# Mixture-of-experts layer, one core: the shared layer of the first four token tiles moved into the second router's tail, in plain fp32

## The chip, the cores and the metric

One core of a Trainium2 chip runs the whole program. The metric is the device time of one execution in microseconds (us), lower is better. TensorE is called PE here, its weight loads PEld, VectorE DVE, ScalarE ACT, GpSimd POOL and SyncE SP. PE's clock has two levels, 2.4 GHz (the profile writes 1.00) and 1.2 GHz (0.50).

## The reference

The input is 16 images of 16 x 16 pixels with 256 channels, so 4096 tokens. Four residual layers follow one another: a spectral mix, a first mixture of experts (gated, top 2 of 8), an attention-like convolution, and a second mixture of experts. Only the last one is touched:

```python
# h: the normalised tokens, 4096 x 256
logits = x @ w_router.T                          # 8 experts
expert_weight, expert_idx = top_k(softmax(logits), 2)
...
inter = square(relu(binned @ w1[e].T))           # each chosen expert, 256 hidden
moe_out = ...scatter of (inter @ w2[e].T) * expert_weight...
sh = square(relu(h @ ws1.T))                     # shared layer, 512 hidden, every token
shared_out = sh @ ws2.T
x = x + shared_out + moe_out
```

## The kernel before

Tokens are held in 32 tiles of 128 rows. `x_res` keeps the residual in SBUF (128 x 256 floats a tile, `x_tile(j)`), and the normalised tokens are written to DRAM twice: as rows (`h_rows`) and turned, channels on partitions (`h_turned`, `ht_dram`). The attention stage writes both, and ends at about 798 us of the profile. From there to the end the kernel has three parts, each a block of its own with a barrier of all engines at its end.

**The second router's tail** (`router_tail("moe1", ...)`, L425 to L543). DVE selects the two best experts, counts tokens per expert, and gives every (token, choice) a slot. Then a loop over 8 batches of 4 tiles and 2 choices builds the table that says which token sits in which slot: DVE compares against a ramp (L527, L529), ACT scales the tile part with the token number (L468, 64 instructions of 128 x 72), and PE adds up 64 products of 128 x 128 by 72 columns in `ids_ps` (L482). Rings are two deep: DVE waits for `s_spread` of two batches before, ACT for `s_equal`, PE for `s_one_hot`. L485 closes the sum, L541 and L543 turn it into integers. SP has one job here, `late`: the load of the 2 MB `down1_raw` (L2382). Before the loop PE does three small products (L475 to L477), and then waits for ACT.

**The second experts** (`mlp("experts1", ...)`), 71 slots of 128 rows. At its start SP loads the first two groups of turned tokens for the part after it (L871), and at its end PE does the first two products of the shared layer (`SharedLead.EARLY`).

**The shared layer and the output** (`SharedLead` L849 and `shared` L899). Every operand is split in a high and a low fp32r half, and each product is made as three (`product`, L176, whose matmuls are L182 to L184). Tokens go in groups of 4 tiles: SP loads 512 KB of `h_turned` a group (L871), ACT and DVE split it (L879, L187), PE projects it in 4 products of 512 columns (6 matmuls each), ACT applies relu, square and the copy of the high half (L966, L968, L972), DVE makes the low half (L187), and PE projects back tile by tile (12 matmuls of 256 columns). PE's order is written out by hand: `project_back(t)`, then `project(t + LEAD)`, with `LEAD = 6`; `project_back(t)` waits until `add_y(t - 4)` has emptied its bank. POOL gathers the two expert rows of each token, two gathers a tile, 64 in all (L923), into a ring of `DEPTH = 8` buffers; a gather waits until the sum of eight gathers before is done. DVE adds the gathers to the residual (`add_routed`, L998, 2 a tile) and then the shared result (`add_y`, L1004). Its order is by hand as well:

```python
for t in range(TILES):
    add_y(t)
    c = t + LEAD
    low_a(c)
    add_routed(t + AHEAD_Y)      # AHEAD_Y = 4
```

SP stores a tile when `add_y` is through (L935). Each DVE wait stands in this order, so a late gather holds up the additions behind it.

Of the kernel before, what the change touches and what calls it, by code (L numbers as in the profile page):

```python
# [23 lines left out]
P = 128  # L24
# [3 lines left out]
KC = C // P  # L28
# [78 lines left out]
def build(nc, A, out):  # L107
    _, where = constants()
    ctx = ExitStack()
    with ctx:  # L110
# [314 lines left out]
        def router_tail(tag, choice, logits, late=None):  # L425

            BATCH = 4
            with ExitStack() as tail:  # L428
# [16 lines left out]
                at_tile = [[sb(f"{tag}_at_tile{k}{b}", [P, BATCH * TABLE_T], HALF, on=tail) for b in range(RING)] for k in range(2)]  # L445
                block = tail.enter_context(nc.Block())
# [7 lines left out]
                if late is not None:  # L454
                    @block.sync
                    def _(sp):
                        late(sp)

                @block.scalar
                def _(act):  # L460
                    act.wait_ge(s["apart"], 1)
                    nc.scalar.activation(share[:, :], apart[:, :], ACT.Exp).then_inc(s["exp"], 1)
                    for n in range(TILES // BATCH):
                        for k in range(2):
                            act.wait_ge(s_equal[k], n + 1)
                            for i in range(BATCH):
                                part = at_tile[k][n % RING][:, i * TABLE_T:(i + 1) * TABLE_T]
                                last = nc.scalar.activation(part, part.bitcast(F32), ACT.Copy, scale=token[:, n * BATCH + i:n * BATCH + i + 1])  # L468
                            last.then_inc(s_one_hot[k], 1)

                @block.tensor
                def _(pe):
                    pe.wait_ge(s["totals"], 1)
                    totals = count[:, :].rearrange("p (e j) -> p e j", e=E)[:, :, TILES - 1]
                    nc.tensor.matmul(sums_ps[:, 0:E], K("before"), totals, start=True, stop=True)  # L475
                    nc.tensor.matmul(sums_ps[:, E:2 * E], K("ones"), totals, start=True, stop=True).then_inc(s["bases"], 1)
                    nc.tensor.matmul(ids_ps[:, :], K("ident"), zeros[:, :], start=True, stop=False)  # L477
                    for n in range(TILES // BATCH):
                        for k in range(2):
                            pe.wait_ge(s_one_hot[k], n + 1)  # L480
                            for i in range(BATCH):
                                last = nc.tensor.matmul(ids_ps[:, :], at_row[k][n % RING][:, i * P:(i + 1) * P],  # L482
                                                        at_tile[k][n % RING][:, i * TABLE_T:(i + 1) * TABLE_T], start=False, stop=False)
                            last.then_inc(s_spread[k], 1)
                    nc.tensor.matmul(ids_ps[:, :], K("ident"), zeros[:, :], start=False, stop=True).then_inc(s["filled"], 1)  # L485
                    pe.wait_ge(s["words"], 1)
                    nc.tensor.matmul(words_ps[0:1, 0:WORDS], etile[:, :], K("words"), start=True, stop=True).then_inc(s["packed"], 1)

                @block.vector
                def _(dve):  # L490
# [40 lines left out]

                    dve.wait_ge(s["exp"], 1)
# [6 lines left out]
                    nc.vector.tensor_scalar(etile[:, :], etile[:, :], float(E - 1), None, ALU.min).then_inc(s["words"], 1)  # L539
                    dve.wait_ge(s["filled"], 1)  # L540
# [308 lines left out]
        class SharedLead:  # L849

            GROUP = 4
            GROUPS = TILES // GROUP
# [12 lines left out]
            def load(self, sp, g):  # L865
                if g >= self.GROUPS:
                    return
                if g >= RING:
                    sp.wait_ge(self.s["h_low"], g - RING + 1)
                width = KC * self.N  # L870
                sp.dma_start(self.hT_raw[g % RING][:, :], ht_dram[:, g * width:(g + 1) * width]).then_inc(self.s_raw[g % RING], 16)  # L871
# [27 lines left out]
        def shared(lead, ws2):  # L899

            GROUP, GROUPS, KI, N = lead.GROUP, lead.GROUPS, lead.KI, lead.N
            LEAD = KI + 2
            DEPTH = 8
            AHEAD_Y = DEPTH // 2
            with ExitStack() as on:  # L905
# [22 lines left out]
                def _(sp):  # L928
                    for g in range(RING, 2 * RING):
                        lead.load(sp, g)  # L930
                    for g in range(GROUPS):
                        lead.load(sp, g + 2 * RING)
                        for t in range(g * GROUP, (g + 1) * GROUP):
                            sp.wait_ge(s["added"], t + 1)
# [4 lines left out]
                def _(pe):  # L939
# [14 lines left out]
                    for t in range(TILES):  # L954
# [25 lines left out]
                def _(dve):  # L980
# [20 lines left out]
                    def add_y(t):  # L1001
                        dve.wait_ge(s["down"], t + 1)
                        dve.wait_ge(s["sum"], t * 2 + 2)
                        nc.vector.tensor_tensor(x_tile(t), x_tile(t), bankY[t % GROUP][:, 0:C], ALU.add).then_inc(s["added"], 1)  # L1004

                    for c in range(LEAD):
                        low_a(c)
                        if c >= LEAD - AHEAD_Y:
                            add_routed(c - LEAD + AHEAD_Y)
                        if c == KI - 1:  # L1010
                            lead.low_h(dve, RING)
                    for t in range(TILES):
# [3 lines left out]
                        add_routed(t + AHEAD_Y)  # L1016
# [1363 lines left out]
        with routing:  # L2380
            router_tail("moe1", choice, by_token(logits1, PARTS[1]),
                        lambda sp: sp.dma_start(down1_raw[0][:, :], A["L1_ffn_w2_stack"]).then_inc(loads["down1"], 16))  # L2382
# [72 lines left out]
```

## Time and profile before

| | us |
|---|---|
| median of 3 runs | 1080.37 (1078.08 to 1084.45) |
| the profiled execution, its own time | 1077.55 |
| its span, first to last instruction | 1075.7 |
| PE, DVE, ACT, POOL busy | 917.6, 609.9, 551.9, 271.2 |

The profile is of one execution. The stages named in the prediction are stretches of its span: the router's tail from 798 to 829 us, the experts from there to about 981, the shared layer from 981 to the end.

### The profile page before, as it was taken

How to read it: one execution, taken by the hardware profiler on the slowest of the kernel's cores; microseconds unless marked ns; L12 is line 12 of the kernel's file. 1: busy time of each engine (PE TensorE's matmuls, PEld its weight loads, DVE VectorE, ACT ScalarE, POOL GpSimd, SP SyncE). 2: the span in 40 equal slices, each digit the busy share in tenths (PEclk: the TensorE clock that was granted, in tenths of full speed). 3: DMA queues.
4: the chain of work that ended last, by engine and by line, in shares of the span. 5: the costliest groups of instructions: out<-in, count | busy, mean ns of one | idle time of the engine just before them, and what ended most of it. 6: DMA issues, size and time to landing. Idle time of an engine off the chain costs nothing. (4 is left out here: it accounts for less than half of the span.)

```text
span 1075.7 us, 20700 instructions
## 1 busy us (share of the span) xinstructions
PE 917.6 (85%) x6102; PEld 785.6 (73%) x6102; DVE 609.9 (57%) x1702; ACT 551.9 (51%) x1372; POOL 271.2 (25%) x274
## 2 busy tenths in 40 slices
PE   5656569999999999997378999998746899998998
PEld 3544458888888888886256777776625899997998
DVE  6887942332323323222777778767768555555786
ACT  6346543443434434343355555554436566667774
POOL 0000031121211212110763220000001544443775
PEclk9858569999999999999589999998655899999999
DMA  9655211111111111111843221102241344444654
GB/s 385 271 193 198 81 40 55 54 55 54 50 54 55 55 54 50 55 44 66 270 128 98 60 79 60 40 21 79 79 157 42 116 138 139 137 133 131 182 163 148
DMA packets 62231, 114.79 MB, mean 107 GB/s; under 512 B 9586, under 2 KB 43012, under 8 KB 60996
## 3 DMA queue, kind: packets, MB, share of 16 engines
q1 hardware_dynamic: 48900, 77.77, 20.5%
q0 software_dynamic: 12960, 35.41, 11.6%
q8 instruction: 58, 0.95, 0.4%
q10 hardware_dynamic: 288, 0.47, 0.1%
q14 instruction: 25, 0.20, 0.1%
HBM read 74.01 MB, written 39.59 MB: 106 GB/s over the span
## 5 line engine op out<-in xcount | busy, mean ns | idle before, releaser
L600 POOL DMA_INDIRECT experts_rows_sb<-h_rows,choices x142 | 137.5, 969 | 651.9 <-POOLq L428 325.9
L799 DVE TENSOR_TENSOR experts_a_sb<-experts_a_sb,experts_bankU 128x512 f32<-128x512 f32 x71 | 48.9, 689 | 223.1 <-PE experts_bankU L184 223.1
L747 ACT ACTIVATE experts_a_sb<-experts_bankG 128x512 f32<-128x512 f32 (+1 forms) x142 | 69.7, 491 | 90.4 <-PE experts_bankG L184 90.3
L760 ACT ACTIVATE experts_y_sb<-experts_bankY 128x256 f32<-128x256 f32 x142 | 54.7, 385 | 86.1 <-PE experts_bankY L181 66.6
L738 ACT ACTIVATE experts_hT<-experts_bankH 128x256 fp32r<-128x256 f32 x142 | 54.2, 382 | 80.5 <-PE experts_bankH L663 80.4
L1198 POOL DMA_INDIRECT attn_y<-y_rows,choices x64 | 65.6, 1024 | 108.3 <-DVE x_res L1652 55.9
L182 PE MATMUL experts_bankY<-down_high,experts_aT 128*128 x284 | 91.5, 322 | 0.3 <-DVE experts_aT L187 0.3
L183 PE MATMUL experts_bankY<-down_low,experts_aT 128*128 x284 | 79.8, 281 | 0.0
L184 PE MATMUL experts_bankY<-down_high,experts_aT 128*128 x284 | 79.8, 281 | 0.0
L923 POOL DMA_INDIRECT shared_y<-y_rows,choices x64 | 67.9, 1061 | 37.8 <-POOLq L555 18.5
L181 PE MATMUL experts_bankY<-down_plain,experts_aT_plain 128*128 x284 | 72.9, 379 | 0.0
L187 DVE TENSOR_TENSOR experts_aT<-experts_bankA,experts_aT 128x256 fp32r<-128x256 f32 x142 | 59.6, 420 | 22.9 <-ACT experts_aT L755 22.9
L670 PE MATMUL experts_bankA<-konst_sb,experts_a_sb 128*128 128x128 f32 x426 | 69.7, 273 | 1.7 <-DVE experts_aT L187 1.7
L663 PE MATMUL experts_bankH<-konst_sb,experts_rows_sb 128*128 128x128 f32 x284 | 55.7, 278 | 16.8 <-issue 14.2
L182 PE MATMUL experts_bankG<-gate_high,experts_hT 128*128 x142 | 69.6, 490 | 0.0
L187 DVE TENSOR_TENSOR experts_hT<-experts_bankH,experts_hT 128x256 fp32r<-128x256 f32 x142 | 59.8, 421 | 9.1 <-ACT experts_hT L738 9.0
L799 DVE TENSOR_TENSOR experts_a_sb<-experts_a_sb,experts_bankG 128x256 f32<-128x256 f32 x71 | 29.9, 421 | 56.1 <-ACT experts_a_sb L747 56.1
L663 PEld LDWEIGHTS experts_bankH<-konst_sb,experts_rows_sb 128*128 128x128 f32 x284 | 37.3, 142 | 27.3 <-issue 18.3
L183 PE MATMUL experts_bankG<-gate_low,experts_hT 128*128 x142 | 56.6, 398 | 0.0
L184 PE MATMUL experts_bankU<-up_high,experts_hT 128*128 x142 | 55.8, 393 | 0.0
L184 PE MATMUL experts_bankG<-gate_high,experts_hT 128*128 x142 | 55.7, 393 | 0.0
L182 PE MATMUL experts_bankU<-up_high,experts_hT 128*128 x142 | 55.6, 392 | 0.0
(367 smaller groups left out, 2626.4 us busy)
## 6 DMA issues: line engine op xcount, KB each, us to landing
y_rows<-experts_y_sb SPq DMA_DIRECT2D x142, 128.0 KB, 1.9
h_rows<-xn SPq DMA_DIRECT2D x32, 256.0 KB, 2.2
mix_xT<-in_xt SPq DMA_DIRECT2D x4, 1024.0 KB, 12.0
x_res<-in_x SPq DMA_DIRECT2D x4, 1024.0 KB, 13.9
gate_raw<-in_L_ffn_gate_w SPq DMA_DIRECT2D x2, 2048.0 KB, 13.6
up_raw<-in_L_ffn_up_w SPq DMA_DIRECT2D x1, 4096.0 KB, 25.1
x_rows<-x_res SPq DMA_DIRECT2D x16, 256.0 KB
x_res<-x_rows SPq DMA_DIRECT2D x8, 512.0 KB, 4.7
```

The source lines that it names most:

```text
L181: return nc.tensor.matmul(out, left[0], right[0], start=start, stop=stop)
L182: nc.tensor.matmul(out, left[0], right[0], start=start, stop=False)
L183: nc.tensor.matmul(out, left[0], right[1], start=False, stop=False)
L184: return nc.tensor.matmul(out, left[1], right[0], start=False, stop=stop)
L187: return eng.tensor_tensor(low, whole, high.bitcast(F32), ALU.subtract)
L600: nc.gpsimd.indirect_dma_start(rows[t % DEPTH][:, :], None, h_dram, bass.IndirectOffsetOnAxis(ap=ids_i[:, t:t + 1], axis=0)).then_inc(s_ro ...
L663: last = nc.tensor.transpose(bankH[:, kc * P:(kc + 1) * P], rows[i % DEPTH][:, kc * P:(kc + 1) * P], K("ident"))
L670: last = nc.tensor.transpose(bankA[:, k * P:(k + 1) * P], a_sb[i % RING][:, k * P:(k + 1) * P], K("ident"))
L747: nc.scalar.activation(a_sb[i % RING][:, :], bankG[i % RING][:, 0:hidden], ACT.Silu if gate is not None else ACT.Relu).then_inc(s["act"], 1)
L799: nc.vector.tensor_tensor(a_sb[i % RING][:, :], a_sb[i % RING][:, :], bankU[i % RING][:, 0:hidden], ALU.mult).then_inc(s["a"], 1)
L923: nc.gpsimd.indirect_dma_start(routed[u % DEPTH][:, :], None, y_dram, bass.IndirectOffsetOnAxis(ap=pos_i[:, t + k * TILES:t + k * TILES + ...
L1198: nc.gpsimd.indirect_dma_start(y_in[u % Y_RING][:, :], None, y_dram, bass.IndirectOffsetOnAxis(ap=pos_i[:, j + k * TILES:j + k * TILES + 1 ...
```

## The change

The four first tiles no longer go through `shared`. A new class `SharedEarly` computes their shared layer inside `router_tail` of the second router, from `h_turned` and from `ws1` and `ws2` in plain fp32 (not split), and adds it to `x_res` there. `shared` then handles 28 tiles; it still gathers and adds the expert rows of all 32 and stores the first four as soon as both sums are done. `AHEAD_Y` goes from 4 to 1, counted now from tile 4, so that DVE adds the expert rows five tiles ahead of the shared result of the same loop index.

```diff
+        class SharedEarly:
+            GROUP = 4
+            KI = IS // P
+            N = GROUP * P
+            PRODUCTS = GROUP * KI
...
+            def load(self, sp):
+                sp.dma_start(self.hT[:, :], ht_dram[:, 0:KC * self.N]).then_inc(self.s["hT"], 16)
+                sp.dma_start(self.ws1[:, :], A["L1_ffn_ws1"]).then_inc(self.s["ws1"], 16)
+                sp.dma_start(self.ws2[:, :], A["L1_ffn_ws2"]).then_inc(self.s["ws2"], 16)
+            def project(self, pe, k):
+                if k == 0:
+                    pe.wait_ge(self.s["hT"], 16)
+                    pe.wait_ge(self.s["ws1"], 16)
+                if k >= RING:
+                    pe.wait_ge(self.s["relu"], k - RING + 1)
+                for kc in range(KC):
+                    last = nc.tensor.matmul(self.bankU[k % RING][:, :], self.ws1[:, kc * IS + k * P:kc * IS + (k + 1) * P],
+                                            self.hT[:, kc * self.N:(kc + 1) * self.N], start=(kc == 0), stop=(kc == KC - 1))
+                last.then_inc(self.s["up"], 1)
+            def project_back(self, pe, first, end):
+                for j in range(first, min(end, self.PRODUCTS)):
+                    t, k = j // self.KI, j % self.KI
+                    if j == 0:
+                        pe.wait_ge(self.s["ws2"], 16)
+                    if t == 0:
+                        pe.wait_ge(self.s["square"], k + 1)
+                    last = nc.tensor.matmul(self.bankY[t // 2][:, t % 2 * C:(t % 2 + 1) * C], self.a[k][:, t * P:(t + 1) * P],
+                                            self.ws2[:, k * C:(k + 1) * C], start=(k == 0), stop=(k == self.KI - 1))
+                    if k == self.KI - 1:
+                        last.then_inc(self.s["down"], 1)
+            def activate(self, act, k):
+                act.wait_ge(self.s["up"], k + 1)
+                nc.scalar.activation(self.a[k][:, :], self.bankU[k % RING][:, :], ACT.Relu).then_inc(self.s["relu"], 1)
+                act.wait_ge(self.s["relu"], k + 1)
+                nc.scalar.activation(self.a[k][:, :], self.a[k][:, :], ACT.Square).then_inc(self.s["square"], 1)
+            def add(self, dve, b):
+                dve.wait_ge(self.s["down"], 2 * b + 2)
+                nc.vector.tensor_tensor(x_tile(2 * b, n=2), x_tile(2 * b, n=2), self.bankY[b][:, :], ALU.add)
...
 SP   +                        if early is not None:
+                            early.load(sp)
                         late(sp)
 ACT, after Exp and before the loop over n
+                        early.activate(act, 0)
+                        early.activate(act, 1)
 ACT, at the end of an iteration
+                        if early is not None and n in (1, 2):
+                            early.activate(act, n + 1)
 PE, after L477 and before the loop
+                        early.project(pe, 0)
+                        early.project(pe, 1)
 PE, at the start of an iteration
+                            if n in (1, 2):
+                                early.project(pe, n + 1)
+                            elif n > 2:
+                                early.project_back(pe, (n - 3) * 4, (n - 2) * 4)
 DVE, after the last comparison                    +  early.add(dve, 0)
 DVE, after L539, before the wait for the table    +  early.add(dve, 1)
...
 class SharedLead
-            GROUPS = TILES // GROUP
+            FIRST = SharedEarly.GROUP
+            GROUPS = (TILES - FIRST) // GROUP
...
 def shared
-            AHEAD_Y = DEPTH // 2
+            AHEAD_Y = 1
 SP
+                    for t in range(FIRST):
+                        sp.wait_ge(s["sum"], t * 2 + 2)
+                        sp.dma_start(out[t * P:(t + 1) * P, :], x_tile(t)).then_inc(s["stored"], 16)
 PE
-                    for t in range(TILES):
+                    for t in range(COUNT):
                         project_back(t)
                         lead.project(pe, t + LEAD)
 DVE
                     for c in range(LEAD):
                         low_a(c)
-                        if c >= LEAD - AHEAD_Y:
-                            add_routed(c - LEAD + AHEAD_Y)
+                        if c >= LEAD - FIRST:
+                            add_routed(c - LEAD + FIRST)
...
-                    for t in range(TILES):
+                    for t in range(AHEAD_Y):
+                        add_routed(FIRST + t)
+                    for t in range(COUNT):
                         add_y(t)
                         c = t + LEAD
                         low_a(c)
-                        add_routed(t + AHEAD_Y)
+                        add_routed(FIRST + t + AHEAD_Y)
```

## Rows read from the trace of the kernel before

**Rows 1.** The page, the span in 40 slices: granted clock of PE in tenths.
```profile
PEclk9858569999999999999589999998655899999999
```
**Rows 2.** Stretch, us; PE, PEld, DVE, ACT, POOL busy; clock, DMA share, GB/s.
```profile
797.00:804.00 7.00, 0.22 (x1) 0.00 (x0) 4.54 (x23) 0.00 (x0) 0.00 (x0) 0.50 0.51 173
...
812.00:828.00 16.00, 15.65 (x65) 14.85 (x65) 14.93 (x36) 15.02 (x62) 0.00 (x0) 0.50 0.00 0
...
836.00:842.00 6.00, 4.66 (x21) 3.86 (x20) 3.10 (x6) 2.87 (x6) 3.33 (x4) 0.50 0.27 70
```
**Rows 3.** Groups of instructions, 795 to 840 us: count, busy us, mean ns, idle before.
```profile
L468 ACT ACTIVATE moe_at_tile<-moe_at_tile,moe_token 128x72 fp32r<-128x72 f32 x64 | 15.8, 339 | 6.5 <-DVE moe_at_row L529 6.5
L482 PE MATMUL moe_ids<-moe_at_tile,moe_at_row 128*128 128x72 f32 x64 | 15.8, 413 | 6.4 <-ACT moe_at_tile L468 6.4
```
**Rows 4.** Timeline of the router's tail: start us, duration us, instruction.
```profile
799.94 0.34 SPq L2382 DMA_DIRECT2D down_raw<-in_L_ffn_w_stack  x1
...
805.32 0.68 PE L477 MATMUL moe_ids<-moe_zeros,konst_sb 128*128 128x72 f32 x2
...
811.21 10.91 ACT L468 ACTIVATE moe_at_tile<-moe_at_tile,moe_token 128x72 fp32r<-128x72 f32 x44 [6.46 <-DVE moe_at_row L529]
...
825.05 0.68 DVE L529 TENSOR_TENSOR moe_at_row<-konst_sb,moe_slot_row 128x512 fp32r<-128x512 f32 x1
...
826.91 0.15 DVE L539 TENSOR_SCALAR moe_etile<-moe_etile 128x1 f32<-128x1 f32 x1
...
828.82 0.15 DVE L543 CAST experts_i<-moe_words 1x9 int32<-1x9 f32 x1
```
**Rows 5.** DMA issues, 799 to 830 us: size of one, median us to landing.
```profile
shared_hT_raw<-h_turned SPq DMA_DIRECT2D x2, 512.0 KB, 4.0
```
**Rows 6.** Timeline, plain fp32 matmuls: at 2.4 GHz (256 columns), at 1.2 GHz (128 columns).
```profile
300.24 1.03 PE L181 MATMUL experts_bankY<-down_plain,experts_aT_plain 128*128 x4
```
```profile
770.76 1.91 PE L1395 MATMUL attn_bankS_along<-end_w,attn_gated 128*128 128x128 f32 x8
```
**Rows 7.** Busy time by stretch where the clock rises and falls again.
```profile
772.00:774.00 2.00, 2.00 (x12) 1.52 (x10) 1.85 (x5) 0.00 (x0) 0.00 (x0) 0.57 0.03 9
774.00:776.00 2.00, 1.18 (x9) 0.79 (x8) 0.95 (x6) 1.06 (x2) 0.00 (x0) 1.00 0.00 0
776.00:778.00 2.00, 1.28 (x20) 1.00 (x20) 1.69 (x10) 0.14 (x1) 0.00 (x0) 0.78 0.52 211
```
**Rows 8.** Groups of instructions, 977 to 1076 us.
```profile
L923 POOL DMA_INDIRECT shared_y<-y_rows,choices x64 | 67.9, 1061 | 37.8 <-POOLq L555 18.5 <-issue 13.4 <-DVE x_res L998 5.8
...
L998 DVE SCALAR_TENSOR_TENSOR x_res<-shared_y,choices,x_res 128x256 f32<-128x256 f32 x64 | 31.0, 484 | 17.3 <-DMA shared_y<-y_rows,choices 15.2
...
L187 DVE TENSOR_TENSOR shared_aT<-shared_a,shared_aT 128x512 fp32r<-128x512 f32 x32 | 22.0, 689 | 11.8 <-ACT shared_aT L972 11.4
L968 ACT ACTIVATE shared_a<-shared_a 128x512 f32<-128x512 f32 x32 | 20.3, 634 | 1.0
```
**Rows 9.** Timeline of PE, two neighbouring starts of a tile's back projection.
```profile
1057.58 0.28 PE L182 MATMUL shared_bankY<-ws,shared_aT 128*128 128x256 f32 x1
...
1060.40 0.28 PE L182 MATMUL shared_bankY<-ws,shared_aT 128*128 128x256 f32 x1
```
**Rows 10.** Timeline of POOL: the first, one long and the last gather.
```profile
982.27 0.94 POOL L923 DMA_INDIRECT shared_y<-y_rows,choices  x1 [18.55 <-POOLq L555]
```
```profile
1013.33 1.64 POOL L923 DMA_INDIRECT shared_y<-y_rows,choices  x1 [0.30 <-DVE x_res L998]
```
```profile
1068.45 0.95 POOL L923 DMA_INDIRECT shared_y<-y_rows,choices  x1 [0.30 <-issue]
```
**Rows 11.** Timeline of DVE: beside the long gather, and at the end.
```profile
1012.93 1.22 DVE L187 TENSOR_TENSOR shared_hT<-shared_hT_raw,shared_hT 128x1024 fp32r<-128x1024 f32 x1
```
```profile
1071.25 0.48 DVE L998 SCALAR_TENSOR_TENSOR x_res<-shared_y,choices,x_res 128x256 f32<-128x256 f32 x1 [0.61 <-DMA shared_y<-y_rows,choices]
1071.65 1.41 DVE L1004 TENSOR_TENSOR x_res<-x_res,shared_bankY 128x256 f32<-128x256 f32 x4
```

More of the change, by code:

```diff
@@ L423, in _, with place @@
                     choice.select(chain, 0, by_pair(logits_ps[0], PARTS[0][1]))
-        def router_tail(tag, choice, logits, late=None):
+        class SharedEarly:
[3 more added lines that the diff above has]
+            PRODUCTS = GROUP * KI
+            def place(self, on):
+                self.s = {n: sem(f"early_{n}") for n in ("hT", "ws1", "ws2", "up", "relu", "square", "down")}
+                self.hT = sb("early_hT", [P, KC * self.N], on=on)
+                self.ws1 = sb("early_ws1", [P, KC * IS], on=on)
+                self.ws2 = sb("early_ws2", [P, self.KI * C], on=on)
+                self.a = [sb(f"early_a{k}", [P, self.N], on=on) for k in range(self.KI)]
+                self.bankU = [pb(f"early_bankU{b}", self.N, on=on) for b in range(RING)]
+                self.bankY = [pb(f"early_bankY{b}", 2 * C, on=on) for b in range(self.GROUP // 2)]
+            def load(self, sp):
[31 more added lines that the diff above has]
+                nc.vector.tensor_tensor(x_tile(2 * b, n=2), x_tile(2 * b, n=2), self.bankY[b][:, :], ALU.add)
@@ L427, in router_tail @@
+        def router_tail(tag, choice, logits, late=None, early=None):
             BATCH = 4
@@ L445, in router_tail @@
                 at_tile = [[sb(f"{tag}_at_tile{k}{b}", [P, BATCH * TABLE_T], HALF, on=tail) for b in range(RING)] for k in range(2)]
+                if early is not None:
+                    early.place(tail)
                 block = tail.enter_context(nc.Block())
@@ L456, in _ @@
                     def _(sp):
+                        if early is not None:
+                            early.load(sp)
                         late(sp)
@@ L462, in _ @@
                     nc.scalar.activation(share[:, :], apart[:, :], ACT.Exp).then_inc(s["exp"], 1)
+                    if early is not None:
+                        early.activate(act, 0)
+                        early.activate(act, 1)
                     for n in range(TILES // BATCH):
@@ L530, in _ @@
                                                     tokens(slot_row, at_j, P), ALU.is_equal).then_inc(s_equal[k], 1)
+                    if early is not None:
+                        early.add(dve, 0)
                     dve.wait_ge(s["exp"], 1)
@@ L539, in _ @@
                     nc.vector.tensor_scalar(etile[:, :], etile[:, :], float(E - 1), None, ALU.min).then_inc(s["words"], 1)
+                    if early is not None:
+                        early.add(dve, 1)
                     dve.wait_ge(s["filled"], 1)
@@ L2381, in build @@
             router_tail("moe1", choice, by_token(logits1, PARTS[1]),
-                        lambda sp: sp.dma_start(down1_raw[0][:, :], A["L1_ffn_w2_stack"]).then_inc(loads["down1"], 16))
+                        lambda sp: sp.dma_start(down1_raw[0][:, :], A["L1_ffn_w2_stack"]).then_inc(loads["down1"], 16), early=SharedEarly())
         with ExitStack() as held:
```

13 lines of the change are left out of this document (8 added, 5 removed).

## The prediction, on record before the change was run

> **What bounds the kernel now.** I read the page's slices of granted clock first, because the change adds PE work: they show 1.2 GHz just ahead of the last quarter, where the second router's tail lies [rows 1]. Then the busy time by stretch: in 797 to 804 us PE does nothing, in 812 to 828 us PE, DVE and ACT are all busy, and the clock stays at 0.50 up to 842 us [rows 2]. The groups of instructions say what that loop is: 64 scalings on ACT in 15.8 us and 64 products on PE in 15.8 us, 0.247 us each, and ACT has no idle time once it has begun [rows 3]. ACT sets the pace, DVE is hardly faster, and PE follows. The whole tail is on the path, since nothing of the experts can start before its table is there.
>
> In the last part the timeline shows PE going from tile to tile in 1060.40 - 1057.58 = 2.82 us [rows 9]. But PE is not alone at the limit. POOL makes 64 gathers from 982.27 to 1068.45 us [rows 10], that is 86.18 / 63 = 1.368 us apart, and between two it rests only the 0.30 us of an issue; its only long idle time, 18.5 us, is ahead of the first [rows 8]. DVE waited 15.2 us in all for gathers to land [rows 8], and the kernel's last additions come behind the last gather [rows 10, 11]. So two queues end together, PE's and POOL's, and the change shortens one.
>
> **The change, part by part.**
>
> *Shared part, PE.* Four tiles fewer are 4 x 2.82 = 11.3 us less of PE [rows 9]. ACT and DVE lose their share of the same work; with them goes one 512 KB load.
>
> *Shared part, POOL.* All 64 gathers stay, and their block starts no sooner. A buffer is freed five PE tiles early now, so POOL waits for no sum, as it hardly did before. What counts is its pace. Its floor is 0.94 + 0.30 = 1.25 us [rows 10], and the mean duration is 1.061 [rows 8] because some gathers are longer. One of 1.64 us began at 1013.33, 0.82 us before the end of a DVE subtraction of two SBUF operands (1012.93 + 1.22), and ended 0.82 us behind it [rows 10, 11]: such a DVE operation in flight delays a gather that starts meanwhile. The Trainium skill, SBUF — State Buffer, section "Who interferes with whom", says of tensor_tensor that with two SBUF inputs it contends only with GpSimd's reads, and infers that it leaves the writing of descriptors alone; by that DVE's work would not touch the pace, which would stay where it is (rival 4), and the row above speaks against it.
> With less PE work DVE will wait for gathers nearly throughout, in step with them. I walked two tiles: a sum starts 2.8 us after its gather (1071.25 us for the one of 1068.45 [rows 10, 11]), the tile's second sum is followed 0.7 us later by the 0.69 us low half [rows 8], and the gather that starts 0.95 us behind the sum meets it and loses 0.35 us; in the next tile the start falls later and loses nothing. One in four loses 0.35: 1.34 us a gather. Some nine gathers at the end meet no low halves (1.25), the first eight take 10.7 us as before: 10.7 + 46 x 1.34 + 9 x 1.25 = 83.6 us, 2.6 less than 86.2. Behind the last gather one addition is left and not three or four: 1.0 us of the 1.41 [rows 11]. Sum of the part: **-3.6 us**. Ends: pace at the floor, 63 x 1.25 = 78.8, gives -7.4 - 1.0 = -8.4; a pace 2 us worse than now gives +1.
>
> *SP in the shared part.* The four early stores come ahead of the load of the fifth group; it is wanted only when four groups are through ACT. Nothing.
>
> *Tail, SP and DMA.* Three issues of 0.33 us go ahead of the 2 MB load, which starts at 800.9 instead of 799.94 [rows 4] and is wanted at 829. Two 512 KB loads issued together land in 4.0 us [rows 5]; issued at 799.94, tokens and `ws1` land by about 805 to 806, when PE is through with its three small products (805.32 + 0.68 [rows 4]). Nothing, at worst 1 us. The store of new semaphores is too small to see.
>
> *Tail, PE.* A plain fp32 matmul is two records. At full clock four records of 256 columns take 1.03 us, of which 0.17 is the drain of the last, so 0.43 us a matmul; at 1.2 GHz eight records of 128 columns take 1.91, also 0.43 us a matmul [rows 6], which is 0.86 us for 256 columns. So `project(k)`, two matmuls of 512 columns, is 1.7 us at full and 3.4 us at half clock, and four steps of `project_back` cost the same. Eight such pieces are added: 13.7 or 27.3 us. The first two fall in PE's idle time from 806 to 812.
>
> *Tail, ACT.* A square of 128 x 512 takes 0.63 us [rows 8] and a relu hardly less, 1.25 us a pair. Four of them are 5.0 us, on the engine that sets the pace. The first two stand **ahead of its whole loop**: at half clock `project(0)` ends at 809.4 and `project(1)` at about 812, so ACT is free at 813.4 and not at 811.21 [rows 4], +2.2; everything of the table is queued behind that wait. The other two add 2.5. So even with PE for nothing the tail grows by 4.7 us.
>
> *Tail, clock.* Before, the loop never raised the clock in 16 us [rows 2]. Dense matmuls raise it: it rose at 773.9 behind some 3.5 us of dense fp32 matmuls, and fell at 777.1 in a stretch with PE busy for 1.2 to 1.3 of 2 us [rows 7]. I expect it up during `project(1)`, and down again soon, since PE then waits two us for ACT. Walked from there, with 0.21 us a table product at half clock (the 0.247 is ACT's) and 0.12 at full: products of batch 0 to 815.9, `project(2)` at half clock to 819.3, batch 1 to 821.0, `project(3)` to 824.4, in which the clock comes up; batch 2 to 825.2; then four times 1.7 + 1.0 us, with a wait for ACT in the first, to 836.1; batch 7 to 837.1. DVE's closing chain, 826.91 + 0.15 - 825.73 = 1.3 us [rows 4], and a first addition now stand behind the last comparison, which waits for PE's batch 5: the end is at 838.3 us, against 828.97 [rows 4]. **+9.4 us.** Ends, by the same walk: clock at full throughout after 811, PE done at 833.6 and the end at 834.9, +6; clock at half throughout, PE done at 849, +21.
>
> *Experts.* They start on a cold PE (0.50 to 842 us, 4.66 us busy of the last 6 [rows 2]). PE idles some 7 us ahead of them in the new kernel too, so the clock will have fallen. Nothing; at best -2.
>
> Sum: 9.4 - 3.6 = **+5.8 us**. On the profiled execution, 1077.55 us, that is 1083.4. The median of the three runs is 2.8 us above it, and I give the time against the median: 1080.4 + 5.8 = **1086.2 us**.
>
> **Rivals.**
> 1. *The clock holds once it is up.* For: at full clock 1.7 of each 2.7 us of the last batches are dense work. Against: the gap behind `project(1)`, and the fall at 777.1 [rows 7]. +6.0 - 3.6 = +2.4: 1082.8 us.
> 2. *The clock stays at half.* For: 16 us of a busy PE didn't raise it [rows 2]. Against: that loop is mostly weight loads of 72 columns each. +21 - 3.6 = +17.4: 1097.8 us.
> 3. *POOL runs at its floor*, the one way to not slower. With fewer low halves and a new rhythm no gather meets a DVE subtraction: -8.4 against +9.4 is +1.0, with rival 1's clock -2.4: 1081.4 or 1078.0 us. It decides once the tail costs less than 8.4 us. For: the first and the last gather take the 0.94 already [rows 10]. Against: DVE will be in step with the gathers.
> 4. *POOL's pace does not improve.* The 11.3 us of PE turn wholly into a wait of DVE for gathers, -1.0 at most: +8.4: 1088.8 us. For: the present pace is only 0.03 us above what my walk gave, and the walk hangs on a phase of 0.1 us. The rule cited above gives the same time, since by it the pace is not DVE's doing.
>
> **How the numbers follow.** Forecast 0.38, rival 1 0.24, rival 2 0.10, rival 3 0.14, rival 4 0.14. A measurement of this kernel can tell about 0.5%, 5.4 us, from no change: 1075.0 to 1085.8. The forecast lies at the upper edge of that, two thirds of it beyond (0.25), rival 2 wholly and rival 4 mostly (0.12) beyond: slower 0.48. Rival 1, most of rival 3 and the rest are within: 0.42. Faster keeps 0.10, for rival 3 with a tail that costs no more than ACT's 4.7. The range leaves out rival 2's upper half and the far end of rival 3: 1077.5 to 1095.5, the likeliest case's own 1083 to 1090.
>
> **What would show each step.** The tail from 799.9 to its last DVE cast: 38 us and not 29. ACT's first scaling at 813.4 and not 811.2. The granted clock in 812 to 826 us: 0.50 for the forecast, 1.00 for rival 1. Last minus first gather: 83.6 us; 79 is rival 3, 86 rival 4. DVE's wait for gathers well above 15.2 us, and PE in the shared part with idle time it didn't have. The forecast is wrong if PE still ends with the last gather, or if the tail grows by less than 5 us or more than 14.

## The result, and the profile after

| | before | after |
|---|---|---|
| median, us | 1080.37 | 1087.07 |
| the profiled execution, own time | 1077.55 | 1089.81 |
| its span | 1075.7 | 1086.9 |
| router's tail, first DVE reduction of its block to its last cast | 28.99 | 36.13 |
| experts, end of the tail to the shared part's first gather | 153.30 | 155.93 |
| shared part, first gather to the end | 93.43 | 92.31 |
| last minus first gather | 86.18 | 85.87 |

Ratio 1.0058, 95% interval 1.003 to 1.0086: slower, and by the 0.5% that the prediction took for what a measurement of this kernel can tell, just beyond it; the interval lies wholly above 1, but its lower end is below that 0.5%. One of the five executions of the changed kernel (1136.13 us, mean granted clock 0.794 and not 0.90) was disturbed and is left out of the ratio. The profiled execution was the slowest of the others; 2.55 us of the 11.2 us by which its span is longer lie ahead of the tail, where nothing was changed. The stages account for the rest: +7.1, +2.6, -1.1. They add up to 8.65 us and the medians differ by 6.7, since the profiled execution lies 2.8 us below its median before and 2.7 us above it after; which stage differs in the other executions is not known.

The slices of granted clock are nearly those of [rows 1]. What differs is in the stretches. Busy time by stretch of the changed kernel: length, PE, PEld, DVE, ACT, POOL busy; clock, DMA share, GB/s.

```profile
807.00:811.00 4.00, 4.00 (x10) 2.45 (x11) 2.82 (x12) 0.23 (x1) 0.00 (x0) 0.50 1.06 450
811.00:818.00 7.00, 4.32 (x16) 2.30 (x15) 6.79 (x18) 5.76 (x18) 0.00 (x0) 0.99 0.24 103
818.00:825.00 7.00, 7.00 (x17) 3.78 (x15) 2.62 (x5) 3.81 (x13) 0.00 (x0) 0.51 0.00 0
825.00:840.00 15.00, 12.87 (x85) 11.68 (x83) 10.72 (x27) 12.19 (x43) 0.43 (x1) 1.00 0.01 1
```

Beside [rows 2] the loop is no longer all at 0.50. The clock rises at 811, falls at 818, and is back at 825: the rise, fall and rise that the forecast walked. The timeline of the tail, PE, then ACT, then SP's issues, says what stood where (start, duration, instruction):

```profile
808.34 5.05 PE L453 MATMUL early_bankU<-early_hT,early_ws 128*128 128x512 f32 x8
815.73 0.64 PE L553 MATMUL moe_ids<-moe_at_tile,moe_at_row 128*128 128x72 f32 x4 [2.33 <-ACT moe_at_tile L529]
...
817.18 2.97 PE L453 MATMUL early_bankU<-early_hT,early_ws 128*128 128x512 f32 x4
819.16 2.54 PE L553 MATMUL moe_ids<-moe_at_tile,moe_at_row 128*128 128x72 f32 x8
821.50 3.60 PE L453 MATMUL early_bankU<-early_hT,early_ws 128*128 128x512 f32 x4
824.28 1.65 PE L553 MATMUL moe_ids<-moe_at_tile,moe_at_row 128*128 128x72 f32 x8
...
828.89 1.97 PE L464 MATMUL early_bankY<-early_ws,early_a 128*128 128x256 f32 x8
...
831.51 1.97 PE L464 MATMUL early_bankY<-early_ws,early_a 128*128 128x256 f32 x8
```
```profile
814.60 4.03 ACT L529 ACTIVATE moe_at_tile<-moe_at_tile,moe_token 128x72 fp32r<-128x72 f32 x16
820.18 0.60 ACT L471 ACTIVATE early_a<-early_bankU 128x512 f32<-128x512 f32 x1 [1.56 <-PE early_bankU L453]
```
```profile
early_ws<-in_L_ffn_ws SPq DMA_DIRECT2D x2, 512.0 KB, 5.0
...
early_hT<-h_turned SPq DMA_DIRECT2D x1, 512.0 KB, 3.8
```

PE waits 2.33 us for ACT's first scaling; at the end of that stretch the clock falls, and the third projection (817.18), the batch behind it and the fourth projection (821.50, 3.60 us) run at 1.2 GHz. From 828.89 a batch takes 2.62 us. The loads landed in 3.8 and 5.0 us, and PE went from its small products straight into the first projection.

In the shared part the two groups that answer to [rows 8], and the last gather and addition that answer to [rows 10, 11]:

```profile
L1000 POOL DMA_INDIRECT shared_y<-y_rows,choices x64 | 67.6, 1057 | 39.3 <-POOLq L630 20.1 <-issue 15.2 <-DVE x_res L1078 4.0
...
L1078 DVE SCALAR_TENSOR_TENSOR x_res<-shared_y,choices,x_res 128x256 f32<-128x256 f32 x64 | 31.1, 486 | 19.7 <-DMA shared_y<-y_rows,choices 17.2 <-DVE x_res L1078 0.5
```
```profile
1080.46 0.95 POOL L1000 DMA_INDIRECT shared_y<-y_rows,choices  x1 [0.30 <-issue]
```
```profile
1083.24 0.48 DVE L1078 SCALAR_TENSOR_TENSOR x_res<-shared_y,choices,x_res 128x256 f32<-128x256 f32 x1 [0.74 <-DMA shared_y<-y_rows,choices]
1083.83 0.42 DVE L1084 TENSOR_TENSOR x_res<-x_res,shared_bankY 128x256 f32<-128x256 f32 x1
```

The mean gather took 1057 ns, as against 1061; POOL's queue is as long as it was, and the end follows it by 1086.9 - 1080.46 = 6.4 us and not 7.25. The forecast took 11.3 us from PE, and they bought 1.1.

### The profile page after: what moved, and what is told of

Same layout as the page of the kernel before. It is cut to its first block and busy times, and to the rows that moved or that the text cites. A ratio compares the mean times of both kernels' runs of the same rounds, so it can differ in the third digit from the quotient of the medians.

```text
span 1086.9 us, 20623 instructions
## 1 busy us (share of the span) xinstructions
PE 924.0 (85%) x6078; PEld 784.1 (72%) x6078; DVE 608.7 (56%) x1695; ACT 548.5 (50%) x1367; POOL 271.1 (25%) x274
## 5 line engine op out<-in xcount | busy, mean ns | idle before, releaser
L1000 POOL DMA_INDIRECT shared_y<-y_rows,choices x64 | 67.6, 1057 | 39.3 <-POOLq L630 20.1
L187 DVE TENSOR_TENSOR experts_aT<-experts_bankA,experts_aT 128x256 fp32r<-128x256 f32 x142 | 59.6, 420 | 23.0 <-ACT experts_aT L830 23.0
L187 DVE TENSOR_TENSOR experts_hT<-experts_bankH,experts_hT 128x256 fp32r<-128x256 f32 x142 | 59.8, 421 | 9.1 <-ACT experts_hT L813 9.1
```

Source lines behind the costliest of these rows:

```text
L187: return eng.tensor_tensor(low, whole, high.bitcast(F32), ALU.subtract)
L1000: nc.gpsimd.indirect_dma_start(routed[u % DEPTH][:, :], None, y_dram, bass.IndirectOffsetOnAxis(ap=pos_i[:, t + k * TILES:t + k * TILES + ...
```

## The experiments

Where no number of executions is given, a time is that of one execution with its profile, and it is read by its stages. A table of them stands at the end of this section. In the diffs, which are put in short, lines with + are the experiment's.

**The tail alone.** The early layer as changed, with the shared part of the kernel before, so the four tiles are computed and added twice.

```diff
-class SharedLead, shared: FIRST = 4, AHEAD_Y = 1
+class SharedLead, shared: as in the kernel before
```

> The changed router tail alone, with the shared part of the kernel before (32 tiles), so the first four tiles get their shared result twice. The tail, from its first DVE operation to its last cast, took 29.0 us before and 36.1 us after the change. Theory (the early work costs what the changed kernel shows): 36 us again, and everything behind it as long as before: first gather to the end of the span 93.4 us. Rival (part of the loss lies in what the early work does to later stages, the clock at the start of the experts or at their end): the stretch from the first expert gather to the first shared gather is 155.0 us as after the change and not 152.4 as before.

1093.5 us. The tail took 38.99 us, ACT's scalings began 13.58 us into it (forecast: 13.4), and the shared part 95.95, no shorter than before. Both are above what was expected (36 and 93.4), and the stretch between the first gathers, 155.45 us, is the rival's. So the tail is a cost by itself, +10.0 here and +7.1 in the changed kernel, with the same instructions. Here the clock rose 11.7 us into the tail, in the second projection; in the changed kernel it was up 8.6 us in, before that projection began.

**The shared part alone.** No early layer, so the first four tiles lack their shared layer.

```diff
-        ... loads["down1"], 16), early=SharedEarly())
+        ... loads["down1"], 16))
```

> The shared part of the changed kernel alone; the early shared layer of the first four tiles is left out, so they lack it. Theory (POOL's 64 gathers bound the part): first gather to the end of the span 92.3 us as after the change, against 93.4 before, and last minus first gather about 86 us; the tail 29.0 us. Rival (my own recorded forecast, DVE in step with the gathers): 90 us and 83.6. Rival (the work of PE bounds it): 82 us.

1076.47 us; shared part 91.82, gathers 85.33. The other half of the change is worth 1.6 us, not 3.6.

**Eight gathers fewer.** As the run before, and the expert rows of the first four tiles are neither gathered nor added; `AHEAD_Y` is 4 again, and the stores of these tiles wait for nothing.

```diff
-                    for t in range(TILES):
+                    for t in range(FIRST, TILES):
                         for k in range(2):
```

> The same with the 8 gathers and additions of the first four tiles left out as well (they get neither expert rows nor shared result), 56 gathers for 28 tiles, with the order of the kernel before. Theory (POOL bound): another 8 x 1.36 = 10.9 us less, first gather to the end of the span 81 to 83 us. If the gathers were not the bound, it stays near 92.

1071.0 us; shared part 83.99, another 7.8 less, of the 8 x 1.25 = 10.0 us that eight gathers take at the floor. DVE's wait for gathers fell to 8.7 us. That is 1 us above the expected 81 to 83, and far from the 92 of a part that gathers don't bound: with 64 gathers it is POOL that sets the part's length. With 56 PE is at the limit too: its last product ends 3.5 us ahead of the end, as in the kernel before (3.6), and not 10.9 as in the run with 64.

**Squares in PSUM.** As the shared part alone, and ACT writes the square over the projection in PSUM, so that the low half (L187) reads one operand from SBUF and one from PSUM. ACT's copy of the high half reads PSUM as well, and a bank is free for the next projection only behind the low half.

```diff
-    nc.scalar.activation(a[k][:, :], a[k][:, :], ACT.Square)
+    nc.scalar.activation(bankU[k][:, :], a[k][:, :], ACT.Square)
...
-    low_half(nc.vector, aT[g % RING][1][:, part], a[k][:, :], ...)
+    low_half(nc.vector, aT[g % RING][1][:, part], bankU[k][:, :], ...)
```

> shared_only with the squares of the shared layer written to PSUM, so that the subtraction of 128 x 512 has one operand in PSUM and only one in SBUF (the arithmetic is the same). Theory (a gather that starts while DVE runs an operation on two SBUF operands waits for its end): the mean gather falls from 1.06 us to about 1.00, last minus first gather from 86 to 82 or 83 us, and the part is 3 to 4 us shorter. Rival (gathers are long because of DMA traffic or the ring of the queue, as a page's rule on tensor_tensor would have it): mean gather 1.06 us as before, and no change of the part.

1069.95 us; shared part 87.60, 4.2 less for the same instructions. First a pair of the shared part alone, POOL's timeline and DVE's: the gather starts 0.09 us into a low half from SBUF and lasts 1.42 us, to 0.82 us behind the low half's end (1007.72 + 0.69).

```profile
1007.81 1.42 POOL L1000 DMA_INDIRECT shared_y<-y_rows,choices  x1 [0.30 <-issue]
```
```profile
1007.72 0.69 DVE L187 TENSOR_TENSOR shared_aT<-shared_a,shared_aT 128x512 fp32r<-128x512 f32 x1
```

With the square in PSUM, a gather that starts 0.35 us into a low half lasts its 0.94 us, and the group's mean is 982 ns:

```profile
1011.21 0.94 POOL L1001 DMA_INDIRECT shared_y<-y_rows,choices  x1 [0.30 <-issue]
```
```profile
1010.86 0.69 DVE L187 TENSOR_TENSOR shared_aT<-shared_bankU,shared_aT 128x512 fp32r<-128x512 f32 x1 [0.58 <-ACT shared_aT L1053]
```
```profile
L1001 POOL DMA_INDIRECT shared_y<-y_rows,choices x64 | 62.8, 982 | 37.8 <-POOLq L630 18.6 <-issue 15.5 <-DVE x_res L1079 3.7
...
L1079 DVE SCALAR_TENSOR_TENSOR x_res<-shared_y,choices,x_res 128x256 f32<-128x256 f32 x64 | 31.0, 485 | 7.2 <-DMA shared_y<-y_rows,choices 4.1
```

Counted over the timelines of both runs, a gather took more than 0.97 us only where it started during a DVE operation of two SBUF operands: 20 of 64 in the shared part alone, 8 with the edit. What they took above 0.946 us adds up to 6.5 and 2.3 us, and the difference, 4.3 us, is what the part lost. With the square in PSUM 13 gathers started during a low half, and none took over 0.95 us. So the length of the gathers follows the operand, and not the DMA traffic: the transfers are the same in both.

**ACT's early work inside the loop.** The changed kernel, with ACT's four pairs behind the scalings of batches 0 to 3, none ahead of the loop, and the back projections one batch later.

```diff
-    early.activate(act, 0); early.activate(act, 1)     (ahead of the loop)
-    if early is not None and n in (1, 2): early.activate(act, n + 1)
+    if early is not None and n < 4: early.activate(act, n)
```

> The changed kernel with ACT's four relu and square pairs inside the loop, one behind each of the batches 0 to 3 (none ahead of the loop), and the back projection one batch later. Theory (part of the tail's cost is the table queued behind ACT's wait for the first products): ACT's loop begins 11.2 us into the tail as before the change (12.1 in the changed kernel), and the tail takes 34 to 36 us instead of 36 to 39. Rival (PE's added work alone sets the tail): no shorter than 36 us.

1092.32 us. ACT's scalings began 11.23 us in, as before the change, and yet the tail took 39.12:

```profile
818.00:825.00 7.00, 4.64 (x25) 3.20 (x24) 4.74 (x11) 6.94 (x24) 0.00 (x0) 0.95 0.00 0
825.00:832.00 7.00, 7.00 (x23) 6.10 (x24) 3.45 (x7) 5.51 (x22) 0.00 (x0) 0.50 0.00 0
```

While ACT was full (6.94 of 7 us) PE had 4.64 us of work, and behind it the clock was down for some 10 us. The theory's 34 to 36 us missed, the rival's "no shorter than 36" held: an early start of ACT's loop does not by itself shorten the tail. The edit also puts PE's back projections later, the last of them into the last batch, so it doesn't price the delay alone.

**No squares early** (relu only, and PE waits for the relu, so the early layer lacks its square), and **no back projection early** (neither it nor its additions).

```diff
-    nc.scalar.activation(self.a[k][:, :], self.a[k][:, :], ACT.Square).then_inc(self.s["square"], 1)
```

> The changed kernel without the four squares of the early part (the first four tiles get a wrong shared result), 4 x 0.63 = 2.5 us less on ACT and nothing else. If ACT bounds the tail: 33.5 us and less. If PE does: 35.5 to 38.5 us, at most 1 us less than with them.

```diff
-    elif n > 2:
-        early.project_back(pe, (n - 3) * 4, (n - 2) * 4)
```

> The changed kernel without the early back projection and its two additions (the first four tiles lack their shared result): 6.8 us of PE at full clock less. If PE bounds the tail: about 32 to 34 us. If ACT does: 34 us and more, since its 64 scalings and four pairs are all there.

1088.64 and 1088.41 us; tails 37.66 and 38.27. Without squares ACT has 2.5 us less; without the back projections PE has 6.8 us less at full clock. Both stay in between the two kernels with everything (36.1 and 39.0). By what was expected the first speaks for PE as the bound (35.5 to 38.5) and the second for ACT (34 and more, where PE would give 32 to 34), so the two together name neither. The rows of the second show why:

```profile
825.00:832.00 7.00, 5.14 (x20) 3.33 (x20) 3.40 (x8) 5.14 (x19) 0.00 (x0) 0.74 0.00 0
832.00:840.00 8.00, 8.00 (x34) 7.62 (x34) 6.09 (x17) 6.60 (x27) 0.00 (x0) 0.50 0.00 0
```

With no back projections among the last batches, PE ran them at 0.50. Less work, slower clock, nearly the same time.

**PE kept busy.** The changed kernel with seven fp32 products of 512 columns into a spare bank, read by nobody.

```diff
+    early.fill(2)                       (before the wait for the counts)
     early.project(pe, 0); early.project(pe, 1)
+    early.fill(2)
...
+    if n == 0 and k == 1 or n in (2, 3) and k == 0:
+        early.fill(1)
     pe.wait_ge(s_one_hot[k], n + 1)
```

> The changed kernel with seven more fp32 products of 512 columns on PE in the router's tail, written to a spare bank that nobody reads: two before PE waits for the counts, two behind the second early projection, one in front of the second choice of batch 0, one in front of the first choice of batches 2 and 3. They put dense work where PE otherwise waits or does 72-column products, and by themselves cost PE time: at full clock 0.85 us each. Theory (the clock decides how long the tail is): the granted clock is at full from about 812 us on and the tail ends earlier although PE has more to do, 34 to 35.5 us against 36.1 (the changed kernel) and 39.0 (tail alone). Rival A (ACT and the waits decide): the added products lengthen the tail, 38 to 41 us. Rival B (filling does not hold the clock): the clock falls as before and the tail grows by twice the fillers in the loop, 41 to 44 us.

1089.43 us; tail 35.81, just above the theory's 34 to 35.5. ACT's scalings began 13.58 us in and the clock rose 11.7 us in, both as in the tail-alone run, and that run's 38.99 is the one to compare with: 3.2 us less with 6 us more work. From 814.7 us to the end the clock was 1.00, but PE was without a gap from 818 on and paid for the last two products.

**Squares in PSUM with the change**, 12 executions. The diff is that of the squares above.

> The changed kernel, with ACT's squares written to PSUM over the projection they come from, so that DVE's low half of the hidden layer reads one operand from SBUF and not two. Theory (a gather that starts while DVE works on two SBUF operands is delayed, and POOL's 64 gathers set the pace of the shared part): the mean gather goes from 1.057 to about 0.99 us and the shared part from 92.3 to 87.6 to 88.5 us, the whole time some 4 us below the changed kernel, 1082 to 1083, and still above the kernel before by 0.2%, for the tail keeps its 7 to 10 us. Rival (the shared part is set by ACT and PE): no change of the part, 92 us, and 1087.

1084.6 us, ratio 1.0039 (1.0019 to 1.006). Mean gather 1019 ns, shared part 89.93: 2.4 us less than the changed kernel, the theory's direction and somewhat over half its size; DVE still waited 14.0 us for gathers. The tail was 36.22.

**Both**, 12 executions: squares in PSUM, and the fillers without those in batches 2 and 3.

```diff
-    if n == 0 and k == 1 or n in (2, 3) and k == 0:
+    if n == 0 and k == 1:
```

> The changed kernel with the squares in PSUM (as in the run before that had them) and five of the seven added products: two before the counts, two behind the second early projection, one in batch 0; the two in batches 2 and 3 are left out. In the run with seven the clock stayed at full from 814.7 us to the tail's end, PE had no idle time from 818 on, and the tail took 35.81 us. Theory (from 820 us on the early products themselves keep the clock up, and the last two fillers only cost their 0.85 us each): clock at full to the end, tail 34 to 34.5 us, whole time 1.5 to 2 us below the changed kernel with the squares in PSUM (ratio to before 1.002 to 1.003). Rival (without them the clock falls between 818 and 825 us, as in the changed kernel): tail 36 to 38.5 us, ratio 1.004 to 1.006.

1081.29 us, ratio 1.0009 (0.9994 to 1.0024). The tail took 33.46 us, below the theory's own 34:

```profile
811.00:818.00 7.00, 6.39 (x24) 3.17 (x22) 6.20 (x14) 5.63 (x19) 0.00 (x0) 1.00 0.03 12
818.00:825.00 7.00, 6.37 (x37) 4.88 (x36) 4.94 (x10) 6.93 (x24) 0.00 (x0) 1.00 0.00 0
825.00:832.00 7.00, 7.00 (x43) 6.38 (x42) 5.33 (x12) 6.38 (x27) 0.00 (x0) 1.00 0.01 2
```

Beside the changed kernel's 4.32 us busy in 811 to 818, PE has 6.39, and the 0.51 of 818 to 825 is 1.00. The twelve executions agree: their mean granted clock is 0.902 to 0.908, as against 0.895 to 0.904 in those with the squares in PSUM alone. What is left of the tail's growth, 33.46 - 28.99 = 4.5 us, is near ACT's 5 us of relus and squares, and ACT is busy 6.93 of 7 us in 818 to 825; but in 825 to 832 PE is the one without a gap, so it isn't shown which of the two sets the rest. The two fillers that were left out don't explain all of the 2.35 us to the run with seven: 1.64 us of them is that ACT's scalings began 11.94 us in here and 13.58 there, since the clock had risen 8.4 us in and not 11.7.

**Squares in PSUM in the kernel before**, 12 executions, nothing of the change.

> The kernel before with nothing but the squares in PSUM (as in low_psum). Theory (PE and POOL ended together before, so relief for one of them shows little): mean gather 1.00 us, the last gather well ahead of PE's end, and 0 to 2 us less in all, not the 4.2 us that the same edit gave with 28 tiles. Rival (POOL alone bounded the part before): 4 us less.

1076.44 us, ratio 0.9973 (0.9954 to 0.9991). It is the fastest complete kernel, ahead of both. The profiled shared part is 1.4 us shorter, within the theory's 0 to 2; the ratio stands for 2.9 us (1.0 to 5.0) and can't tell the theory from the rival's 4. Gathers 81.82 us, but the end now comes 10.2 us behind the last, and DVE waits 9.0 us for gathers: PE, with all 32 tiles, does its last product 2.6 us before the end and sets it.

**High copies of the first group on DVE**, 12 executions, on top of the last.

```diff
+    if g == 0: return                                  (ACT: no copy)
+    if g == 0:                                         (DVE)
+        dve.wait_ge(s["square"], c + 1)
+        nc.vector.tensor_copy(aT[0][0][:, part], bankU[k][:, :])
```

> The kernel before, with the squares in PSUM as above (all 32 tiles in the shared part, nothing of the change), and in the first group of the shared part DVE makes the high copies of the four hidden blocks instead of ACT. At the start of the part PE waits for ACT's chain of relu, square and copy; with the copies on DVE the first back projection should start some 1.8 us sooner. Theory (PE ends last in that version, 10.2 us behind the last gather): the end comes 1 to 1.8 us sooner, 1074.7 to 1075.5, ratio to the kernel before 0.995 to 0.9965. Rival (the delay at the start is made good elsewhere, or the low halves are late instead): no change against 1076.4, ratio 0.997 to 0.998.

1077.7 us, ratio 0.998 (0.9962 to 0.9999): no gain, the rival's result. The fourth block's copy stood on DVE behind two expert additions:

```profile
988.77 1.08 DVE L1006 SCALAR_TENSOR_TENSOR x_res<-shared_y,choices,x_res 128x256 f32<-128x256 f32 x2
989.77 0.68 DVE L992 CAST shared_aT<-shared_bankU 128x512 fp32r<-128x512 f32 x1
```

The first back projection began 7.14 us behind the first gather as against 7.25, and the clock dipped in 990 to 996 us, to a mean of 0.72. The shared part was 1.5 us longer than without the edit; how much of it is the dip is not shown.

| profiled run, us | tail | experts | shared part | gathers |
|---|---|---|---|---|
| before | 28.99 | 153.30 | 93.43 | 86.18 |
| after | 36.13 | 155.93 | 92.31 | 85.87 |
| tail alone | 38.99 | 156.36 | 95.95 | 88.76 |
| shared part alone | 28.97 | 153.17 | 91.82 | 85.33 |
| eight gathers fewer | 28.99 | 152.90 | 83.99 | 76.80 |
| squares in PSUM, shared part alone | 28.99 | 152.75 | 87.60 | 81.09 |
| ACT's work inside the loop | 39.12 | 156.03 | 93.26 | 86.83 |
| no squares early | 37.66 | 154.62 | 91.61 | 85.21 |
| no back projection | 38.27 | 153.03 | 93.03 | 86.58 |
| PE kept busy | 35.81 | 156.12 | 92.55 | 86.11 |
| squares in PSUM, change | 36.22 | 154.16 | 89.93 | 83.49 |
| both | 33.46 | 155.30 | 89.88 | 83.45 |
| squares in PSUM, before | 28.98 | 153.49 | 92.03 | 81.82 |
| high copies on DVE, before | 28.99 | 153.06 | 93.50 | 81.35 |

The table shows how far one profile can be trusted. The shared part of the changed kernel stands in it six times with the same instructions (after, shared part alone, ACT's work inside the loop, no squares, no back projection, PE kept busy): 91.6 to 93.3 us. The tail of the changed kernel stands in it three times: 36.13, 36.22 and 38.99.

## Why the prediction was right

The forecast of 1086.2 us met 1087.07, +5.8 against +6.7, and the class with the highest chance (slower, 0.48) came true, by the prediction's own limit of 0.5%. The direction rests on a mechanism that the runs bear out: a tail that grows by more than POOL lets the shared part shrink. That the sum came so close is in part luck: its terms missed by 2 to 3 us each, in both directions.

**Tail, +9.4: right in its mechanism.** Measured +7.1 in the changed kernel and +10.0 with the tail alone. The prices held: 1.7 us for a projection at full clock and 3.4 at half (ACT's first relu starts at 811.72, 3.4 us behind 808.34), 2.62 us a late batch for a forecast 2.7, no wait for the loads, the first addition behind the last comparison. The 2.3 us between forecast and result are the moment at which the clock moved: it was up before the second projection began, so ACT's scalings started 12.07 us in where I had 13.4, and it fell only when the third had begun (2.97 us for it, where I had 3.4).

**Tail, ACT alone +4.7: half right.** As a size it is near: with the clock held the tail grows by 4.5. But there ACT's loop begins 0.7 us late and not 2.2, so the 4.5 isn't made up as I had it. But "ahead of its whole loop" was not where the cost lay. With the loop started as early as before, the tail was 39.12 us. In the changed kernel PE's late batches, 2.62 us each with hardly a gap, end the tail.

**Rival 1 (the clock holds)** did not happen by itself, and where dense products were added to make it hold, the tail went to 33.46: +4.5, and 1.5 below the walk's +6. **Rival 2** did not happen: no run with the early layer whole stayed at half.

**Experts, nothing: a miss of 2.6 us.** The expected low clock at their start was there, but the tail's kernels also lose time at the other end of the stage. Where the experts pass into the shared part, PE idles, and in some profiles the clock then falls. Stretches of the changed kernel, and of the one with squares in PSUM:

```profile
986.00:988.00 2.00, 1.11 (x8) 0.97 (x8) 2.00 (x5) 0.97 (x2) 0.00 (x0) 1.00 0.19 66
988.00:990.00 2.00, 1.71 (x9) 1.59 (x9) 0.21 (x1) 0.65 (x2) 0.00 (x0) 0.67 0.19 66
990.00:992.00 2.00, 2.00 (x6) 1.58 (x5) 0.00 (x0) 0.12 (x1) 0.00 (x0) 0.50 0.19 66
```
```profile
986.00:988.00 2.00, 1.71 (x13) 1.53 (x13) 0.90 (x2) 0.77 (x2) 0.00 (x0) 1.00 0.00 0
988.00:990.00 2.00, 2.00 (x11) 1.58 (x10) 0.00 (x0) 0.39 (x1) 0.00 (x0) 1.00 0.38 131
```

The runs with that dip (after, tail alone, ACT's work inside, PE kept busy) have 155.93 to 156.36 us; the two with the early layer whole and no dip have 154.16 (shown) and 155.30, and the one without squares, which has none either, 154.62. So the dip may take a part, 0.6 to 2 us. The rest is there before the dip: the last of the experts' row gathers starts 133.82 us into the stage before the change, 134.87 in the changed kernel, and 0.8 to 1.4 us later than before in every profile with the early back projections. It is not there in the kernel without them (133.49; 153.03 in all). Why is open; no run took it apart.

**Shared part, -3.6: the term that was mis-sized.** Measured -1.1 in the changed kernel, -1.6 with the rest taken away, -1.0 in the mean of the six profiles; against one profile of before and a spread of 1.7 us, none of these is exact, but none of the six comes near the forecast's 89.8 us. The end after the last gather came 0.8 us nearer (forecast 1.0). But "one in four loses 0.35: 1.34 us a gather" gave 83.6 us for the gathers, and they took 85.87 (85.2 to 86.8 in the six): rival 4's pace. The walk of two tiles took a steady phase, in which one gather in four is delayed by 0.35 us. In the changed kernel's trace 23 of 64 are, by 0.31 us in the mean, 7.1 us in all; before the change it was 25 and 7.3 us. The loss hardly changed, though there was less DVE work. Nor did DVE come to wait for gathers "nearly throughout": 17.2 us for 15.2. What lay behind the walk, that DVE's operations of two SBUF operands delay gathers, was right: moving one of them to PSUM took 66 ns from each gather (1048 to 982) and 4.2 us from the part. The Trainium skill, SBUF — State Buffer, section "Who interferes with whom", infers that a tensor_tensor leaves the writing of descriptors alone, and the prediction took from it a pace that isn't DVE's doing (rival 4); here the measurement decides against that reading. The same section says that a DVE instruction with two SBUF inputs contends with GpSimd instructions that read SBUF, and the gather does read its row numbers (`choices`) there, so the runs may agree with that sentence; no run separates the reading from the writing. **Rival 3** (the floor, -8.4) did not happen; with that edit and no early layer the part came to 87.60, -5.8.

**The signs that were named.** The tail grew by 7.1 us, within the 5 to 14 that it was allowed, and PE no longer ended with the last gather: its last product ends 10.9 us before the end, the last gather starts 6.4 before it. The gathers' 86 us was the sign of rival 4, which came true for that part; its whole time, 1088.8, missed by the tail that it shared with the forecast. The granted clock fits neither sign: 0.99 in 811 to 818 us and 0.51 in 818 to 825, where the forecast's sign was 0.50 all through 812 to 826, though its walk had the rise and the fall in it.

So the change took 11.3 us of PE (by the forecast's price) from a part that POOL's 64 gathers bound, and put 13.7 us (at full clock) where PE, ACT and the clock bound. The sum of the terms came out near the measured one because an overpriced tail (-2.3) stood against an overpriced gain (+2.5), and the experts' 2.6 us, which I did not have, make most of what the profiled stages (+8.7) show above the forecast.

## What to carry to other kernels

Before work is taken out of a stage to shorten it, count the queue that would end next: here 64 gathers with 0.30 us between them took back most of an expected gain. Work put into the gaps of a slow loop is priced at the clock that it gets, and a wait of some two microseconds for another engine was followed by its fall; five products that nobody reads, put into such gaps, cost less than nothing. Look at the operands' memories too: one result written to PSUM and not to SBUF brought the kernel before down by 0.3% (0.1 to 0.5), and beat both kernels.

## What the runs showed of the hardware that was not expected

- A gather that starts during a DVE operation of two SBUF operands ends 0.82 us behind that operation's end; with one operand in PSUM it takes its 0.94 to 0.95 us. I had this from one row; that it holds for the 512-column low half, and that it was worth 4.2 us, came from the runs. There are exceptions. Where the operation is nearly over, the gather takes 0.94 to 0.95 us as always (a low half with 0.01 us to go). And in the shared part alone the three gathers that started 3 to 10 ns into a low half took 0.95 us; the next, at 52 ns, took 1.46.
- Less PE work did not shorten the tail (38.27 us without the back projections), and more PE work did (33.46 us with five added products), with the granted clock at 0.50 through the last batches of the one and at 1.00 in the other.
- The same instructions took 36.13, 36.22 and 38.99 us in the tail, as the clock rose 8.6, 8.8 or 11.7 us into it. A difference of 3 us in this stage, between two profiles, tells nothing by itself: the single profiles of the experiments on the tail are to be read by their rows, beside the moment at which the clock rose.
